# Third attention: TensorE's sums placed later by the number of units that VectorE takes

## The chip, the cores and the metric

The kernel runs on one core of a Trainium2 chip (trn2). The metric is the device time of one execution in microseconds, here the median of three runs; lower is better. One further execution was recorded by the hardware profiler, and all rows below are of that one.

## The reference

The reference is a chain of eight layers on an activation of 4 batches x 1024 tokens x 128 channels in float32. The seventh layer, the third attention, is the one that the change acts on. It has 16 heads of 8 channels, and its queries and keys are the same centred tokens:

```python
xh = x.reshape(B, T, H, hd)
x_centered = xh - jnp.mean(xh, axis=1, keepdims=True)
corr = jnp.einsum('bthd,bThd->bhtT', x_centered, x_centered)
corr = jax.nn.softmax(corr, axis=-1)
out = jnp.einsum('bhtT,bThd->bthd', corr, xh)
```

The first and the third layer are attentions too (one with a slope bias on the scores, one with scores damped by distance); the others are feed-forward layers and a layer of fast weights. Each layer is added to the activation.

## The kernel before

The whole chain is one program; each layer is a block in which every engine has its own instruction stream, and streams meet only through semaphores. All three attentions use `attend_transposed` when the scores are small enough (the third one always).

**Units and places.** The 16 heads are taken in 4 head groups (`HG`) of 4 heads (`GH`), for each of 4 batches. Within a head group there are 8 key tiles `J` of 128 keys (`JT`), so 32 units (`UNITS`); unit n = 4J + j is head j against key tile J, a tile of 128 keys x 1024 queries. `ORDER` says which unit stands at which place of the program. In the third attention `given=(31,)`: unit 31 is not exponentiated by ScalarE but computed by VectorE as a power of two (a range split and a polynomial, `take_power`, `round_power`, `raise_two`), and it stands at place 2. So units 0 and 1 are at places 0 and 1, and unit n from 2 to 30 is at place n + 1.

**TensorE.** `scores(hg, place, b)` (L995, matmuls at L1012) writes a unit's scores, two matmuls of 512 queries that run side by side, into one of three slots of PSUM (`s_ps`, `SLOTS = 3`), place modulo 3 over the batch's 128 places. It waits for the exponential of the unit that held the slot (`exped`), or for `powers_out` where that was VectorE's unit. As 128 is not a multiple of 3, the first three places of a batch take the slots of the last group's places 30, 31 and 29, in this order. `sum_up(hg, J, c, b)` (L1017, matmuls at L1036) multiplies the four tiles of key tile J by the values, for query half c (0 left, 1 right), and accumulates in `o_ps`; in the profile it is eight matmuls. The left half of J waits for the exponentials of all four units. For J = 0 both halves wait until VectorE has taken the last head group's sums out of `o_ps` (`o_out`), for J = 7 the left half waits for VectorE's unit (`raised_out`).

TensorE's order is written out by hand in `batch` (L1045): at each n from 0 to 31 it issues the scores of place n + 3 (of the next head group or batch from n = 29 on), and then, before the change,

```python
if n % GH == GH - 1:
    sum_up(hg, n // GH, 0, b)
if n % GH == 1:
    if n > GH:
        sum_up(hg, n // GH - 1, 1, b)
```

that is, the left half of J at n = 4J + 3 and the right half at n = 4J + 5; the right half of J = 7 comes at n = 1 of the next head group. Batch 0 and batch 3 are written out, batches 1 and 2 are a loop of the engine (`pe.Fori`).

**ScalarE.** `batch` (L1116) takes the places in order, one `Exp` of 128 x 1024 each (L1129), from `s_ps` into `probs`, which holds two key tiles (`J % 2`). Before the first unit of a key tile (j = 0) it waits for `summed`, which the right half of the sum of the key tile two back increments:

```python
if j == 0:
    act.wait_ge(summed, b * (HG * JT) + (hg * JT + J + 1))
```

`summed` starts at 2. For J = 0 of a head group this is the last head group's J = 6, for J = 1 it is its J = 7.

**VectorE** takes the next head group's unit out of its slot (`take_power`, L1174), copies the left and the right sums out of `o_ps` (`take_sums`, L1153) when `left_summed` and `summed` allow, and raises its unit. **GpSimd** copies the values of each head group (`v_set`) and scales finished batches. **SyncE** loads the queries and keys of the next head group after a count of `exped` and moves sums to DRAM.

Of the kernel before, what the change touches and what calls it, by code (L numbers as in the profile page):

```python
# [20 lines left out]
P = 128  # L21
D = 128
BATCH, SEQ = 4, 1024
# [769 lines left out]
def attend_transposed(nc, tag, V, operands, joined, ident, table=None, slopes=None, span=None, X=None, w_out=None,  # L793
# [10 lines left out]
    NB = HG * UNITS  # L804
    SLOTS = 3
    TAKE_AT = (4, 7)
    ORDER = [n for n in range(UNITS) if n not in given]
    KEPT = len(ORDER)
    NE = HG * KEPT
    NG = len(given)  # L810
    GIVEN_AT = (2, 15)[:NG]
    for place, n in zip(GIVEN_AT, given):
        ORDER.insert(place, n)
    RAISE = 7
    LATER = 6
    INVERT_AT = (22, 26)
# [6 lines left out]
    def part(h, J, c):  # L823

        lo, hi = span(h, J)
        lo, hi = max(lo, c * BANK), min(hi, (c + 1) * BANK)
        return (lo, hi) if lo < hi else None

    EARLY = 2 * (BATCH - 1)
    KNOWN = (HG - 1) * GH * HD  # L830
# [7 lines left out]
    with ExitStack() as stack:  # L838
# [7 lines left out]
        w_last = k.sb(f"{tag}_w_last", [P, D])  # L846
        spreader = k.sb(f"{tag}_spreader", [P, P])
        update = k.sb(f"{tag}_update", [P, 2, 4, D])
        if given:
            power = k.sb(f"{tag}_power", [P, SEQ])  # L850
            whole = k.sb(f"{tag}_whole", [P, SEQ], I32)
            raised = k.sb(f"{tag}_raised", [P, NG, SEQ])
            powers_out = k.sem(f"{tag}_powers_out")
            rounded = k.sem(f"{tag}_rounded")
            stepped = k.sem(f"{tag}_stepped")
            doubled = k.sem(f"{tag}_doubled")
            raised_out = k.sem(f"{tag}_raised_out")
# [33 lines left out]
        def _(sp):  # L891
# [32 lines left out]

            def ahead(b, hg):

                sp.wait_ge(exped, b * NE + ((hg - 1) * KEPT + SLOTS + (LATER if hg == 1 else 0)))
                operands.load(sp, hg % HG, b + hg // HG)

            def batch(b, first, final):  # L930
# [60 lines left out]
        def _(pe):  # L991
            pe.sem_inc(summed, 2)

            def scores(hg, place, b):
                J, j = divmod(ORDER[place], GH)  # L995
                half = hg % 2
                if place == 0:
                    pe.wait_ge(loaded[half], b * (HG // 2 * operands.all_in) + (hg // 2 + 1) * operands.all_in)
                at = hg * UNITS + place
                back = at - SLOTS if at >= SLOTS else max(m for m in range(-SLOTS, 0) if slot(0, m + NB) == slot(0, at))  # L1000
                of, was = divmod(back, UNITS)
                if ORDER[was] in given:
                    pe.wait_ge(powers_out, b * (NG * HG) + (of * NG + given.index(ORDER[was]) + 1))
                else:
                    pe.wait_ge(exped, b * NE + (of * KEPT + ORDER[was] + 1 + SLOTS))
                for c in range(2):
                    if not part(hg * GH + j, J, c):
                        continue
                    left, right = part(hg * GH + j, J, c)
                    tile = int(c != J // (JT // 2)) if by_dve else c  # L1010
                    rows = slice(PAIR_ROW * tile, PAIR_ROW * tile + operands.depth(tile))
                    last = pe.matmul(s_ps[:, slot(hg, place), left:right], k_rows[rows, half, j, J * P:(J + 1) * P],  # L1012
                                     q_rows[rows, half, j, left:right], start=True, stop=True)
                last.then_inc(scored, 1)

            def sum_up(hg, J, c, b):
                if J == 0:  # L1017
                    pe.wait_ge(o_out, b * (2 * HG) + (2 * hg + 3 + c))
                if c == 0:
                    if J == 0:  # L1020
                        pe.wait_ge(v_set, b * HG + (hg + 1))
                    pe.wait_ge(exped, b * NE + (hg * KEPT + min(GH * (J + 1), KEPT) + SLOTS))
                    if given and J == JT - 1:
                        pe.wait_ge(raised_out, b * (NG * HG) + (hg + 1) * NG)
                for j in range(GH):
                    h = hg * GH + j
                    meets = [i for i in range(JT) if part(h, i, c)]
                    if J not in meets:
                        continue
                    left, right = part(h, J, c)  # L1030
                    seen = part(h, J - 1, c)[1] if J > meets[0] else left
                    pieces = [(lo, hi) for lo, hi in ((left, min(seen, right)), (seen, right)) if lo < hi]
                    for lo, hi in pieces:
                        n = J * GH + j
                        weights = raised[:, given.index(n), lo:hi] if n in given else probs[:, J % 2, j, lo:hi]
                        last = pe.matmul(o_ps[VW * j:VW * (j + 1), c, lo - c * BANK:hi - c * BANK],  # L1036
                                         v_cols[:, hg % 2, J, j, :], weights,
                                         start=(J == meets[0]),
                                         stop=(J == meets[-1] and hi == right))
                if c == 1:  # L1040
                    last.then_inc(summed, 1)
                elif J == JT - 1:
                    last.then_inc(left_summed, 1)

            def batch(b, first, final):  # L1045
                for hg in range(HG):
                    for n in range(UNITS):
                        m = n + SLOTS
                        if m < UNITS:
                            scores(hg, m, b)  # L1050
                        elif hg + 1 < HG:
                            scores(hg + 1, m - UNITS, b)
                        elif not final:
                            scores(0, m - UNITS, b + 1)

                        if n % GH == GH - 1:
                            sum_up(hg, n // GH, 0, b)
                        if n % GH == 1:
                            if n > GH:
                                sum_up(hg, n // GH - 1, 1, b)  # L1060
                            elif hg:
                                sum_up(hg - 1, JT - 1, 1, b)
                            elif not first:
                                sum_up(HG - 1, JT - 1, 1, b - 1)
                if final:
                    sum_up(HG - 1, JT - 1, 1, b)

            for n in range(SLOTS):
                scores(0, n, 0)
# [42 lines left out]
        def _(act):  # L1112
# [2 lines left out]

            def batch(b):  # L1116
                for hg in range(HG):
                    for place, n in enumerate(ORDER):
                        if n in given:
                            continue  # L1120
                        J, j = divmod(n, GH)
                        lo, hi = span(hg * GH + j, J)
                        if by_dve:
                            act.wait_ge(adjusted, b * NE + (hg * KEPT + n + 1))
                        else:
                            act.wait_ge(scored, b * NB + (hg * UNITS + place + 1))
                        if j == 0:
# [13 lines left out]
        def _(dve):  # L1141
# [29 lines left out]
            def take_power(b, hg, i):  # L1171

                dve.wait_ge(scored, b * NB + (hg * UNITS + GIVEN_AT[i] + 1))
                dve.tensor_scalar(power[:, :], s_ps[:, slot(hg, GIVEN_AT[i]), :], LOG2_E, -126.0,  # L1174
                                  ALU.mult, ALU.max).then_inc(powers_out, 1)

            def round_power(b, hg, i):
                at = b * (NG * HG) + (hg * NG + i)
# [3 lines left out]
                dve.tensor_copy(whole[:, :], power[:, :]).then_inc(rounded, 1)  # L1182

            def raise_two(b, hg, i):
                at = b * (NG * HG) + (hg * NG + i)
                done = b * (NG * HG * RAISE) + (hg * NG + i) * RAISE
                rest, acc = power[:, :], raised[:, i, :]
# [35 lines left out]
            def batch(b, first, final):  # L1223
                for hg in range(HG):
                    if not by_dve:
                        if final and hg == HG - 1:
                            invert(b, 0, 1)
                            invert(b, 1, 1)
                        following = given and not (final and hg == HG - 1)
# [4 lines left out]
                        if following:  # L1234
                            round_power(*after, 0)
                        take_sums(b, hg, 1)
                        if following:
# [4 lines left out]
                        for i in range(1, NG if following else 1):  # L1242
                            take_power(*after, i)
# [17 lines left out]
            for i in range(NG):  # L1261
                take_power(0, 0, i)
                round_power(0, 0, i)
                raise_two(0, 0, i)
# [240 lines left out]
def centred_attention(nc, tag, X, ident, parts_dram, shift_dram, const, head_of):  # L1505
# [6 lines left out]
    with ExitStack() as stack:  # L1512
# [4 lines left out]
        norm_and_centre(nc, f"{tag}_split", X, XN, parts_dram, shift_dram, head_of, operands, ident)  # L1517
        joined = k.sb(f"{tag}_joined", [P, TOK])
        attend_transposed(nc, f"{tag}_att", XN, operands, joined, ident, X=X, kept=const.kept_sums,
                          given=(TPB * GH - 1,))  # L1520


def norm_and_centre(nc, tag, X, XN, parts_dram, shift_dram, head_of, operands, ident):
# [1474 lines left out]
```

## Time and profile before

| | us |
|---|---|
| median of three runs | 3316.86 |
| lowest and highest of them | 3312.75, 3324.0 |
| the profiled execution, its own time | 3323.09 |
| its span, first to last instruction | 3321.4 |
| mean granted TensorE clock over the span | 0.941 |
| third attention, first exponential to last | 2779 to 3244 |

The span is what the rows' times count from. The profiled execution was 6.2 us slower than the median of the runs. PE is TensorE, ACT ScalarE, DVE VectorE, POOL GpSimd, SP SyncE. Exponentials overlap at their edges, so a row that merges several has a length below their sum.

### The profile page before, as it was taken

How to read it: one execution, taken by the hardware profiler on the slowest of the kernel's cores; microseconds unless marked ns; L12 is line 12 of the kernel's file. 1: busy time of each engine (PE TensorE's matmuls, PEld its weight loads, DVE VectorE, ACT ScalarE, POOL GpSimd, SP SyncE). 2: the span in 40 equal slices, each digit the busy share in tenths (PEclk: the TensorE clock that was granted, in tenths of full speed). 3: DMA queues.
4: the chain of work that ended last, by engine and by line, in shares of the span. 5: the costliest groups of instructions: out<-in, count | busy, mean ns of one | idle time of the engine just before them, and what ended most of it. 6: DMA issues, size and time to landing. Idle time of an engine off the chain costs nothing. (4 is left out here: it accounts for less than half of the span.)

```text
span 3321.4 us, 53185 instructions
## 1 busy us (share of the span) xinstructions
PE 2874.0 (87%) x17952; PEld 1294.0 (39%) x17952; DVE 2340.6 (70%) x3805; ACT 2377.6 (72%) x3572; POOL 224.3 (7%) x180
## 2 busy tenths in 40 slices
PE   4888888899999578888889999979979756888886
PEld 2221222666776311111147666732237551111115
DVE  6777777677776767777767777779999855443454
ACT  5889889555455679999955555556635657999994
POOL 2000000000000310000010000010000011000002
PEclk8899999999999789999989999989979967999997
DMA  5444552000000544544300000000000004233321
GB/s 130 66 61 59 68 69 42 26 0 1 0 0 1 140 81 59 66 56 65 53 32 0 0 0 0 0 28 1 1 1 0 0 22 104 40 56 47 57 49 28
DMA packets 79832, 125.47 MB, mean 38 GB/s; under 512 B 12984, under 2 KB 32344, under 8 KB 78748
## 3 DMA queue, kind: packets, MB, share of 16 engines
q1 hardware_dynamic: 79612, 122.65, 21.8%
q8 instruction: 125, 2.05, 0.3%
q14 instruction: 95, 0.78, 0.1%
HBM read 87.49 MB, written 29.16 MB: 35 GB/s over the span
## 5 line engine op out<-in xcount | busy, mean ns | idle before, releaser
L1952 ACT ACTIVATE m_mix_hidden<-m_mix_up_ps 128x512 f32<-128x512 f32 x512 | 305.7, 597 | 295.1 <-PE m_mix_up_ps L1868 295.1
L1129 ACT ACTIVATE b_direct_probs<-b_direct_s_ps 128x1024 f32<-128x1024 f32 x512 | 473.6, 1091 | 18.2 <-PE b_direct_o_ps L1036 11.9
L1876 PE MATMUL m_mix_down_ps<-m_w,m_mix_hidden 128*128 128x128 f32 x4096 | 474.8, 276 | 0.0
L1876 PEld LDWEIGHTS m_mix_down_ps<-m_w,m_mix_hidden 128*128 128x128 f32 x4096 | 467.2, 192 | 15.3 <-issue 15.3
L1868 PE MATMUL m_mix_up_ps<-m_mix_ZT,m_w 128*128 128x512 f32 x1024 | 471.8, 619 | 0.0
L1129 ACT ACTIVATE a_direct_probs<-a_direct_s_ps 128x1024 f32<-128x1024 f32 (+10 forms) x512 | 431.8, 938 | 54.7 <-DVE a_direct_s_ps L1167 41.9
L1129 ACT ACTIVATE c_att_probs<-c_att_s_ps 128x1024 f32<-128x1024 f32 x496 | 457.9, 1141 | 6.8 <-PE c_att_s_ps L1012 4.2
L1167 DVE SCALAR_TENSOR_TENSOR a_direct_s_ps<-distance,slopes,a_direct_s_ps 128x512 f32<-128x512 f32 (+3 forms) x512 | 355.3, 732 | 117.7 <-PE a_direct_s_ps L1012 114.7
L1164 DVE TENSOR_TENSOR b_direct_s_ps<-b_direct_s_ps,distance 128x512 f32<-128x512 f32 x512 | 335.8, 695 | 141.9 <-PE b_direct_s_ps L1012 141.0
L1036 PE MATMUL c_att_o_ps<-c_att_probs,c_v_cols 128*32 128x512 f32 x1984 | 274.9, 610 | 50.2 <-ACT c_att_probs L1129 50.2
L1036 PE MATMUL b_direct_o_ps<-b_direct_probs,v_cols 128*32 128x512 f32 x2048 | 275.1, 610 | 14.0 <-DVE b_direct_taken L1153 13.1
L1036 PE MATMUL a_direct_o_ps<-a_direct_probs,v_cols 128*32 128x512 f32 (+12 forms) x2168 | 270.4, 550 | 16.3 <-DVE a_direct_taken L1153 14.9
L1868 PEld LDWEIGHTS m_mix_up_ps<-m_mix_ZT,m_w 128*128 128x128 f32 x1024 | 157.5, 190 | 291.1 <-ACT m_mix_hidden L1952 274.1
L2071 DVE TENSOR_REDUCE m_mix_mixed<-m_mix_weighted 128x128 f32<-128x1024 f32 x128 | 246.9, 1929 | 4.4
L1012 PE MATMUL b_direct_s_ps<-b_q_rows,b_k_rows 48*128 48x512 bf16 x1024 | 198.3, 392 | 47.5 <-ACT b_direct_probs L1129 15.7
L1012 PE MATMUL a_direct_s_ps<-a_q_rows,a_k_rows 48*128 48x512 bf16 (+13 forms) x984 | 194.2, 380 | 50.1 <-ACT a_direct_probs L1129 22.5
L1174 DVE TENSOR_SCALAR c_att_power<-c_att_s_ps 128x1024 f32<-128x1024 f32 x16 | 19.6, 1225 | 237.7 <-PE c_att_s_ps L1012 237.7
L1012 PE MATMUL c_att_s_ps<-c_q_rows,c_k_rows 49*128 49x512 bf16 x1024 | 162.7, 388 | 19.2 <-ACTq L1113 11.9
L2068 DVE TENSOR_TENSOR m_mix_weighted<-m_mix_down_ps,m_mix_combine 128x1024 f32<-128x1024 f32 x128 | 156.4, 1222 | 30.0 <-PE m_mix_down_ps L1876 24.6
L1012 PEld LDWEIGHTS b_direct_s_ps<-b_q_rows,b_k_rows 48*128 48x128 bf16 x1024 | 47.7, 93 | 332.7 <-ACT b_direct_probs L1129 321.0
L1012 PEld LDWEIGHTS a_direct_s_ps<-a_q_rows,a_k_rows 48*128 48x128 bf16 (+1 forms) x984 | 46.7, 94 | 289.5 <-ACT a_direct_probs L1129 261.2
L2330 DVE TENSOR_TENSOR f_recur_dots_prods<-f_recur_dots_vecs 128x1024 f32<-128x1024 f32 (+2 forms) x128 | 153.8, 1216 | 0.0
(385 smaller groups left out, 3498.5 us busy)
## 6 DMA issues: line engine op xcount, KB each, us to landing
qk_parts<-b_qkv_parts SPq DMA_DIRECT2D x48, 256.0 KB, 3.5
qk_parts<-a_qkv_parts SPq DMA_DIRECT2D x24, 256.0 KB, 4.9
a_k_rows<-qk_parts SPq DMA_DIRECT2D x32, 192.0 KB
a_q_rows<-qk_parts SPq DMA_DIRECT2D x32, 192.0 KB
b_k_rows<-qk_parts SPq DMA_DIRECT2D x32, 192.0 KB
b_q_rows<-qk_parts SPq DMA_DIRECT2D x32, 192.0 KB
qk_parts<-c_split_parts SPq DMA_DIRECT2D x24, 256.0 KB, 3.0
c_k_rows<-qk_parts SPq DMA_DIRECT2D x32, 192.0 KB
```

The source lines that it names most:

```text
L1012: last = pe.matmul(s_ps[:, slot(hg, place), left:right], k_rows[rows, half, j, J * P:(J + 1) * P], q_rows[rows, half, j, left:right], star ...
L1036: last = pe.matmul(o_ps[VW * j:VW * (j + 1), c, lo - c * BANK:hi - c * BANK], v_cols[:, hg % 2, J, j, :], weights, start=(J == meets[0]), ...
L1129: act.activation(probs[:, J % 2, j, lo:hi], s_ps[:, slot(hg, place), lo:hi], ACT.Exp).then_inc(exped, 1)
L1164: ins = dve.tensor_tensor(held, held, near, ALU.mult)
L1167: ins = dve.scalar_tensor_tensor(out=held, in0=near, scalar=slopes[:, h:h + 1], in1=held, op0=ALU.mult, op1=ALU.add)
L1174: dve.tensor_scalar(power[:, :], s_ps[:, slot(hg, GIVEN_AT[i]), :], LOG2_E, -126.0, ALU.mult, ALU.max).then_inc(powers_out, 1)
L1868: pe.matmul(up_ps[:, f % UP_BANKS, :], w["w1"][:, f * P:(f + 1) * P], ZT[:, half, :], start=True, stop=True).then_inc(up_done, 1)
L1876: last = pe.matmul(down_ps[:, t % 2, e, :], hidden[:, e * HALVES + h, t * P:(t + 1) * P], w["w2"][:, e * HALVES + h, :], start=(h == 0), s ...
L1952: act.activation(hidden[:, f, :], up_ps[:, f % UP_BANKS, :], ACT.Silu).then_inc(silu_done, 1)
L2068: dve.tensor_tensor(weighted[:, :, :], down_ps[:, t % 2, :, :], over(combine[:, half, t, :], D), ALU.mult).then_inc(down_out, 1)
L2071: dve.tensor_reduce(mixed[:, :], weighted[:, :, :].rearrange("p e d -> p d e"), AX, ALU.add).then_inc(summed, 1)
L2330: dve.tensor_tensor(prods[:, r % 2, at + lo:at + hi, :], vecs[:, r % 2, lo:hi, :], vecs[:, r % 2, other:other + 1, :].to_broadcast([P, hi ...
```

## The change

Two things are done to `attend_transposed`. First, the units given to VectorE may differ from head group to head group (`given` is a tuple of tuples), with the counts of semaphores taken from running sums (`KEPT`, `GIVEN`); the third attention passes unit 31 for each of the four head groups, and the other two pass none. With these arguments every count comes out as before, and VectorE's program is the same. Second, `sums_at` places TensorE's sums: the halves of J stand at n = 4J + 3 + g and 4J + 5 + g, where g is the number of units that the head group gives to VectorE. That is 1 in the third attention and 0 in the others. So in the third attention the left halves move from n = 4J + 3 to 4J + 4 and the right halves from 4J + 5 to 4J + 6; the two halves of J = 7 stand at n = 0 and n = 2 of the next head group (after the last batch they are issued at the end).

```diff
-    ORDER = [n for n in range(UNITS) if n not in given]
-    KEPT = len(ORDER)
-    NE = HG * KEPT
-    NG = len(given)
-    GIVEN_AT = (2, 15)[:NG]
-    for place, n in zip(GIVEN_AT, given):
-        ORDER.insert(place, n)
+    given = given or ((),) * HG
+    GIVEN_AT = (2, 6)
+    ORDER = [[n for n in range(UNITS) if n not in units] for units in given]
+    KEPT = [sum(len(order) for order in ORDER[:hg]) for hg in range(HG + 1)]
+    NE = KEPT[HG]
+    GIVEN = [sum(len(units) for units in given[:hg]) for hg in range(HG + 1)]
+    NG = GIVEN[HG]
+    for order, units in zip(ORDER, given):
+        for place, n in zip(GIVEN_AT, units):
+            order.insert(place, n)
...
+    def sums_at(hg, n):
+
+        return [(past, J, c) for past in (1, 0) for J in range(JT) for c in range(2)
+                if n + past * UNITS == J * GH + (GH - 1, GH + 1)[c] + len(given[(hg - past) % HG])]
...
-                        if n % GH == GH - 1:
-                            sum_up(hg, n // GH, 0, b)
-                        if n % GH == 1:
-                            if n > GH:
-                                sum_up(hg, n // GH - 1, 1, b)
-                            elif hg:
-                                sum_up(hg - 1, JT - 1, 1, b)
+                        for past, J, c in sums_at(hg, n):
+                            if hg >= past:
+                                sum_up(hg - past, J, c, b)
                             elif not first:
-                                sum_up(HG - 1, JT - 1, 1, b - 1)
+                                sum_up(HG - 1, J, c, b - 1)
                 if final:
-                    sum_up(HG - 1, JT - 1, 1, b)
+                    for n in range(GH + 2):
+                        for past, J, c in sums_at(HG, n):
+                            if past:
+                                sum_up(HG - 1, J, c, b)
...
         attend_transposed(nc, f"{tag}_att", XN, operands, joined, ident, X=X, kept=const.kept_sums,
-                          given=(TPB * GH - 1,))
+                          given=((TPB * GH - 1,),) * (HEADS // GH))
```

## Rows read from the trace of the kernel before

**Rows 1.** Page, first part: busy time, share, instructions of each engine.
```profile
PE 2874.0 (87%) x17952; PEld 1294.0 (39%) x17952; DVE 2340.6 (70%) x3805; ACT 2377.6 (72%) x3572; POOL 224.3 (7%) x180
```
**Rows 2.** Busy time by stretch: us, each engine, PEclk, DMA share, GB/s.
```profile
2779.00:3244.00 465.00, 407.54 (x3058) 79.54 (x3058) 211.76 (x214) 458.08 (x498) 25.49 (x18) 0.99 0.32 50
```
**Rows 3.** Page, costliest groups: busy, mean ns; idle before, releaser.
```profile
L1129 ACT ACTIVATE c_att_probs<-c_att_s_ps 128x1024 f32<-128x1024 f32 x496 | 457.9, 1141 | 6.8 <-PE c_att_s_ps L1012 4.2
...
L1036 PE MATMUL c_att_o_ps<-c_att_probs,c_v_cols 128*32 128x512 f32 x1984 | 274.9, 610 | 50.2 <-ACT c_att_probs L1129 50.2
```
**Rows 4.** Timeline of ScalarE, third attention: start, length, merged instructions, idle before.
```profile
2785.62 1.94 ACT L1129 ACTIVATE c_att_probs<-c_att_s_ps 128x1024 f32<-128x1024 f32 x2 [0.83 <-PE c_att_s_ps L1012]
2788.25 107.13 ACT L1129 ACTIVATE c_att_probs<-c_att_s_ps 128x1024 f32<-128x1024 f32 x116 [0.68 <-PE c_att_s_ps L1012]
...
3011.26 1.94 ACT L1129 ACTIVATE c_att_probs<-c_att_s_ps 128x1024 f32<-128x1024 f32 x2 [0.59 <-PE c_att_o_ps L1036]
3015.12 3.77 ACT L1129 ACTIVATE c_att_probs<-c_att_s_ps 128x1024 f32<-128x1024 f32 x4 [1.93 <-PE c_att_s_ps L1012]
3019.68 108.96 ACT L1129 ACTIVATE c_att_probs<-c_att_s_ps 128x1024 f32<-128x1024 f32 x118 [0.79 <-PE c_att_s_ps L1012]
3129.23 114.62 ACT L1129 ACTIVATE c_att_probs<-c_att_s_ps 128x1024 f32<-128x1024 f32 x124 [0.59 <-PE c_att_o_ps L1036]
```
**Rows 5.** ScalarE's timeline, single exponentials: places 29, 30, 31, then 0', 4', 5'.
```profile
3039.60 1.28 ACT L1129 ACTIVATE c_att_probs<-c_att_s_ps 128x1024 f32<-128x1024 f32 x1
3040.50 1.29 ACT L1129 ACTIVATE c_att_probs<-c_att_s_ps 128x1024 f32<-128x1024 f32 x1
3041.44 1.27 ACT L1129 ACTIVATE c_att_probs<-c_att_s_ps 128x1024 f32<-128x1024 f32 x1
3042.68 1.02 ACT L1129 ACTIVATE c_att_probs<-c_att_s_ps 128x1024 f32<-128x1024 f32 x1
...
3045.43 1.02 ACT L1129 ACTIVATE c_att_probs<-c_att_s_ps 128x1024 f32<-128x1024 f32 x1
3046.50 1.02 ACT L1129 ACTIVATE c_att_probs<-c_att_s_ps 128x1024 f32<-128x1024 f32 x1
```
**Rows 6.** TensorE's timeline at the same seam; the 3042.77 row from a narrower window.
```profile
3041.01 0.61 PE L1012 MATMUL c_att_s_ps<-c_q_rows,c_k_rows 49*128 49x512 bf16 x4
3041.54 1.07 PE L1036 MATMUL c_att_o_ps<-c_att_probs,c_v_cols 128*32 128x512 f32 x8
3042.54 0.61 PE L1012 MATMUL c_att_s_ps<-c_q_rows,c_k_rows 49*128 49x512 bf16 x4
3042.77 0.38 PE L1012 MATMUL c_att_s_ps<-c_q_rows,c_k_rows 49*128 49x512 bf16 x2
...
3044.99 0.63 PE L1036 MATMUL c_att_o_ps<-c_att_probs,c_v_cols 128*32 128x512 f32 x3
...
3045.99 0.61 PE L1012 MATMUL c_att_s_ps<-c_q_rows,c_k_rows 49*128 49x512 bf16 x4
```
**Rows 7.** VectorE's timeline at the same seam: the first step on its unit.
```profile
3043.19 1.23 DVE L1174 TENSOR_SCALAR c_att_power<-c_att_s_ps 128x1024 f32<-128x1024 f32 x1 [16.04 <-PE c_att_s_ps L1012]
```
**Rows 8.** Timelines of ScalarE (place 31) and TensorE, seam from batch 1 to 2.
```profile
3009.40 1.27 ACT L1129 ACTIVATE c_att_probs<-c_att_s_ps 128x1024 f32<-128x1024 f32 x1
3009.81 0.39 PE L1012 MATMUL c_att_s_ps<-c_q_rows,c_k_rows 49*128 49x512 bf16 x2 [0.45 <-ACT c_att_probs L1129]
3010.13 1.07 PE L1036 MATMUL c_att_o_ps<-c_att_probs,c_v_cols 128*32 128x512 f32 x8
...
3014.70 0.61 PE L1012 MATMUL c_att_s_ps<-c_q_rows,c_k_rows 49*128 49x512 bf16 x4 [1.97 <-issue]
```
**Rows 9.** Busy time by stretch as in rows 2, and one sum at its start.
```profile
2779.00:2788.00 9.00, 7.60 (x36) 1.02 (x32) 8.15 (x9) 7.72 (x10) 0.00 (x0) 0.52 0.22 44
...
3011.00:3020.00 9.00, 7.03 (x48) 1.19 (x48) 5.99 (x8) 6.03 (x7) 1.23 (x1) 0.81 0.01 4
2783.11 1.94 PE L1036 MATMUL c_att_o_ps<-c_att_probs,c_v_cols 128*32 128x512 f32 x8 [0.40 <-ACT c_att_probs L1129]
```

More of the change, by code:

```diff
@@ L848, in attend_transposed @@
         update = k.sb(f"{tag}_update", [P, 2, 4, D])
-        if given:
-            power = k.sb(f"{tag}_power", [P, SEQ])
+        if NG:
+            power = k.sb(f"{tag}_power", [P, max(len(units) for units in given), SEQ])
             whole = k.sb(f"{tag}_whole", [P, SEQ], I32)
-            raised = k.sb(f"{tag}_raised", [P, NG, SEQ])
+            raised = k.sb(f"{tag}_raised", [P, max(len(units) for units in given), SEQ])
             powers_out = k.sem(f"{tag}_powers_out")
@@ L925, in ahead @@
             def ahead(b, hg):
[L927 removed]
+                sp.wait_ge(exped, b * NE + (KEPT[hg - 1] + SLOTS + (LATER if hg == 1 else 0)))
                 operands.load(sp, hg % HG, b + hg // HG)
@@ L994, in scores @@
             def scores(hg, place, b):
-                J, j = divmod(ORDER[place], GH)
+                J, j = divmod(ORDER[hg][place], GH)
                 half = hg % 2
@@ L1001, in scores @@
                 of, was = divmod(back, UNITS)
-                if ORDER[was] in given:
-                    pe.wait_ge(powers_out, b * (NG * HG) + (of * NG + given.index(ORDER[was]) + 1))
+                unit = ORDER[of][was]
+                if unit in given[of]:
+                    pe.wait_ge(powers_out, b * NG + (GIVEN[of] + given[of].index(unit) + 1))
                 else:
-                    pe.wait_ge(exped, b * NE + (of * KEPT + ORDER[was] + 1 + SLOTS))
+                    pe.wait_ge(exped, b * NE + ((KEPT[of] if of >= 0 else KEPT[HG - 1] - NE) + unit + 1 + SLOTS))
                 for c in range(2):
@@ L1021, in sum_up @@
                         pe.wait_ge(v_set, b * HG + (hg + 1))
-                    pe.wait_ge(exped, b * NE + (hg * KEPT + min(GH * (J + 1), KEPT) + SLOTS))
-                    if given and J == JT - 1:
-                        pe.wait_ge(raised_out, b * (NG * HG) + (hg + 1) * NG)
+                    pe.wait_ge(exped, b * NE + (min(KEPT[hg] + GH * (J + 1), KEPT[hg + 1]) + SLOTS))
+                    if given[hg] and J == JT - 1:
+                        pe.wait_ge(raised_out, b * NG + GIVEN[hg + 1])
                 for j in range(GH):
@@ L1034, in sum_up @@
                         n = J * GH + j
-                        weights = raised[:, given.index(n), lo:hi] if n in given else probs[:, J % 2, j, lo:hi]
+                        weights = raised[:, given[hg].index(n), lo:hi] if n in given[hg] else probs[:, J % 2, j, lo:hi]
                         last = pe.matmul(o_ps[VW * j:VW * (j + 1), c, lo - c * BANK:hi - c * BANK],
@@ L1117, in batch @@
                 for hg in range(HG):
-                    for place, n in enumerate(ORDER):
-                        if n in given:
+                    for place, n in enumerate(ORDER[hg]):
+                        if n in given[hg]:
                             continue
@@ L1123, in batch @@
                         if by_dve:
-                            act.wait_ge(adjusted, b * NE + (hg * KEPT + n + 1))
+                            act.wait_ge(adjusted, b * NE + (KEPT[hg] + n + 1))
                         else:
@@ L1173, in take_power @@
                 dve.wait_ge(scored, b * NB + (hg * UNITS + GIVEN_AT[i] + 1))
-                dve.tensor_scalar(power[:, :], s_ps[:, slot(hg, GIVEN_AT[i]), :], LOG2_E, -126.0,
+                dve.tensor_scalar(power[:, i, :], s_ps[:, slot(hg, GIVEN_AT[i]), :], LOG2_E, -126.0,
                                   ALU.mult, ALU.max).then_inc(powers_out, 1)
             def round_power(b, hg, i):
-                at = b * (NG * HG) + (hg * NG + i)
+                at = b * NG + (GIVEN[hg] + i)
                 dve.wait_ge(powers_out, at + 1)
@@ L1181, in round_power @@
                     dve.wait_ge(raised_out, at)
-                dve.tensor_copy(whole[:, :], power[:, :]).then_inc(rounded, 1)
+                dve.tensor_copy(whole[:, :], power[:, i, :]).then_inc(rounded, 1)
             def raise_two(b, hg, i):
-                at = b * (NG * HG) + (hg * NG + i)
-                done = b * (NG * HG * RAISE) + (hg * NG + i) * RAISE
-                rest, acc = power[:, :], raised[:, i, :]
+                at = b * NG + (GIVEN[hg] + i)
+                done = b * (NG * RAISE) + (GIVEN[hg] + i) * RAISE
+                rest, acc = power[:, i, :], raised[:, i, :]
                 dve.wait_ge(rounded, at + 1)
@@ L1228, in batch @@
                             invert(b, 1, 1)
-                        following = given and not (final and hg == HG - 1)
+                        following = NG and not (final and hg == HG - 1)
                         after = (b, hg + 1) if hg + 1 < HG else (b + 1, 0)
@@ L1236, in batch @@
                         take_sums(b, hg, 1)
+                        for i in range(1, len(given[after[1]]) if following else 1):
+                            take_power(*after, i)
                         if following:
@@ L1241, in batch @@
                             invert(b - 1, 1)
-                        for i in range(1, NG if following else 1):
-                            take_power(*after, i)
+                        for i in range(1, len(given[after[1]]) if following else 1):
                             round_power(*after, i)
@@ L1259, in batch @@
                                 invert(b, INVERT_AT.index(n), 1)
-            for i in range(NG):
+            for i in range(len(given[0])):
                 take_power(0, 0, i)
```

## The prediction

> **What bounds the kernel now.** I read the page first: no engine is busy all the time, TensorE 87%, ScalarE 72% [rows 1], so the stage has to be taken by itself. The diff acts only on the third attention, where units are given to VectorE: the first two pass an empty tuple, for which every place, count and wait works out as before. The third one's exponentials run from 2779 to 3244 us, and there the stretch shows ScalarE busy 458 of 465 us and TensorE 408 at a granted clock of 0.99 [rows 2]. The costliest groups say how the two meet: TensorE's sums sat idle 50.2 us for the exponentials, ScalarE only 6.8 us in all [rows 3]. ScalarE sets the end of this stage; TensorE has room, but it runs in program order, and what stands behind a waiting instruction is late with it.
>
> ScalarE's own timeline has seven gaps that the profile counts [rows 4]. Two (0.83, 0.68) follow the slow first microseconds, two (1.93, 0.79) follow the jump of TensorE's loop, and three (0.59 in the row shown, 0.68, 0.59) stand where a batch begins. All that TensorE's order could give back there is 0.83 + 0.68 + 1.93 + 0.79 = 4.2 us.
>
> The smaller losses don't count as gaps, since exponentials overlap; they show in the ends. Call the places of a head group 0 to 31, the next group's 0' to 31'. Exponentials of places 30 and 31 end at 3041.79 and 3042.71, 0.92 apart, ScalarE's steady pace. That of 0' ends at 3043.70, 0.99 later: 0.07 lost. Those of 4' and 5' end at 3046.45 and 3047.52, 1.07 apart: 0.15 lost [rows 5]. So 0.22 us is lost at each seam between head groups. Why: place 0' is unit 0, which writes the half of `probs` that the sum of J = 6 reads, and it waits for `summed`. The right half of that sum begins at 3041.54 [rows 6], ends 1.07 later, and 0' is dispatched at 3042.68 [rows 5]. Place 5' is unit 4, which waits for the sum of J = 7, begun at 3044.99 and ended near 3046.05, and for its scores, issued behind it at 3045.99 and done 0.39 later [rows 6].
>
> **The change.** Nothing is added or removed in instructions on ScalarE, VectorE, GpSimd or SyncE; the DMAs and their queue's waits get the same counts. Only TensorE's sums move, each half one place later: the left from 4J + 3 to 4J + 4, the right from 4J + 5 to 4J + 6. What each passes is one `scores` (two matmuls) with its wait. For unit 4J + 3, which sits at place 4J + 4, this fits: the left half used to hold back the next scores while it waited, and no longer does. The 50.2 us of idle time before the sums [rows 3] shrink, but that idle time is TensorE's. ScalarE's seven gaps are its only chance to gain.
>
> The price is on the release of `probs`. Steps from the rows: TensorE sees an exponential's end 0.06 us later (3042.71, then scores at 3042.77), a sum is issued 0.31 behind scores (3009.81 to 3010.13), the next issue is 1.00 behind a half sum (3041.54 to 3042.54), scores to scores 0.23 (two places issued from 3042.54, the second at 3042.77), and 0' is dispatched 1.14 behind the half sum's start [rows 5, 6, 8].
>
> *Seam inside a batch (12 of them).* The right half of J = 6 now stands at n = 30, behind the scores of place 33 (1'), which need the slot of place 30: 3041.79 + 0.06 = 3041.85. The half sum goes at 3042.16 instead of 3041.54, and 0' is dispatched at 3043.30 and ends at 3044.32. Without loss it would be 3042.71 + 0.92 = 3043.63: 0.69 lost where 0.07 was. What is late next: scores of 2' go at 3043.16; VectorE's first step on its unit follows 0.43 behind and takes 1.23 [rows 7], so it is done by 3044.82, in time. Scores of 3' wait for 0': 3044.38. The left half of J = 7 now stands behind them, 3044.69. Scores of 4' follow at 3045.69, and 4' is dispatched at 3046.12. With 1' and 3' ending at 3045.24 and 3046.16 (0.92 apart behind 0'), 4' was due by 3046.05 (its end at 3047.07 less 1.02): 0.07 lost. Scores of 5' go at 3045.92, the right half of J = 7 at 3046.23, and 5' is dispatched at 3046.23 + 1.14 = 3047.37, or 0.08 later if its two waits cost what they do now (scores done at 3046.38, dispatch at 3046.50, where 0.04 is usual). Its end at 3048.47 is 0.41 behind 3047.14 + 0.92. The seam loses 0.69 + 0.07 + 0.41 = 1.17 against 0.22, +0.95 with the 0.08 and +0.87 without it; I take +0.93, nearer the former, since the 0.08 is there now. Twelve make **11.2 us**.
>
> *Seam between batches (3).* 128 places on three slots don't divide, so scores of 0' wait there for place 30 and those of 1' for place 31. Before, the right half of J = 6 starts behind the former, at 3010.13, and 0' at 3011.26 [rows 4, 8]. Now it stands behind the latter: place 31 ends at 3010.67, so 3011.04, +0.91. The rest of the seam adds the 0.48 of 4' and 5' for the 0.15 there is now: +1.24 each, **2.5 us** for two. At the third TensorE's loop jumps back, 1.97 us idle behind its last half sum, scores of 3' at 3014.70 [rows 8]. Now the jump stands behind the scores of 2', which slip to 3012.04 and last 0.39; with 1.97 idle the scores of 3' come at 3014.4 or a little later, no later than before, and the 1.93 us gap absorbs the late 0'. But two half sums follow before the scores of 5' and 6' where one did: **+0.7**, with 1.5 either way, since a clock drop falls right there [rows 9]. SyncE's loads for the next head group wait for a count of exponentials and are late only with them.
>
> *Inside a head group (6 sums of 16 groups).* The right half now frees `probs` at E + 0.06 + 0.31 + 1.14 = E + 1.51, where E is the end of place 4J - 2; unit 4J of two tiles on is due to be dispatched at E + 2 x 0.92 - 0.10 = E + 1.73. (0.10 is 1.02 less 0.92.) 0.22 us of room covers it, and I cost it at nothing; if that room is gone, each tenth lost costs 96 x 0.1 = 9.6 us.
>
> *Start and end of the stage.* In the cold first group scores of 7 come sooner, the release of place 9 later: 0.0, within 1. At the end nothing changes: there are no scores left to pass, and both halves of J = 7 wait for the last exponential and follow it as before.
>
> Sum: 11.2 + 2.5 + 0.7 = **+14.4 us**. Against the profiled execution (span 3321.4, its own time 3323.09) that is 3337.5; the three runs' median is 3316.86, 6.2 lower, and I predict against it: **3331.3 us**, 0.43% slower. Bounds: nothing lost but the gaps given back, -4.2; all seams with 1.17 + 0.1 and the interior with a lost tenth, +26.
>
> **The rivals.** *Not slower.* If 0' were held by its scores and not by the sum, the change would only give back gaps: 0 to 4.2 us, 3312.7 to 3316.9. For it: the exponentials' starts run ahead of their ends by up to 0.27 us (1.29 against 1.02 long [rows 5]). Against: 0' starts 0.07 behind the end of the half sum, its scores were issued by 3041.24, and the profile names the sum as releaser at the batch seam [rows 4]. It decides if the half sum can start by 3043.63 - 1.02 - 1.14 = 3041.47; I have 3042.16.
>
> *Only the first wait bites.* If 5' is hidden by what 0' already lost: 12 x 0.62 + 3 x 0.91 = 10.2, less up to 4.2 of gaps: 3323 to 3327. My walk leaves 5' 0.3 short after the earlier delay was counted, which speaks against it.
>
> *The interior stalls too.* If ScalarE's pace is that of its starts, 0.90 us (3039.60 to 3040.50 [rows 5]), the release comes at start + 1.26 + 1.51 = 2.77 against 3 x 0.90 = 2.71. That is 0.06 us lost 96 times, 5 to 6 us more: 3337. For it: the starts do run at 0.90. Against: a duration that grows from 1.02 to 1.29 while ends stay 0.92 apart says the starts run ahead of the work. The Trainium skill, "Perfetto Trace Analysis", section "DVE / Act Engine Instruction", has the profiled start as the moment when the instruction leaves the queue and begins to execute; by that rule this rival would hold, and the growing durations speak against it here.
>
> *The clock falls.* TensorE gets shorter, evenly spread holes in place of one long one. The granted clock is 0.52 in the first 9 us, 0.81 in the 9 us around the loop's jump [rows 9] and 0.99 over the whole [rows 2]; at the lower of its two levels, 1.2 GHz, a sum's eight matmuls take 1.94 us and not 1.07 [rows 6, 9]. Four places would then need about 2 x 1.86 + 4 x 0.4 = 5.4 us where ScalarE needs 3.7: 1.7 us lost per four places, 20 us if one of ten fours fell there, 3351. TensorE's total work is unchanged and each hole gets shorter, so it is unlikely. The Trainium skill, "TensorE: Matmul & The Clock Gate", section "A second HAM failure mode: psum-queue depth-cycling", reports a kernel whose small idles between groups of matmuls let the clock oscillate; the present kernel has such idles and holds 0.99, so the trace doesn't agree so far.
>
> **How the numbers follow.** Chances: forecast 0.70 (3331.3, by itself 3326 to 3336), only the first wait 0.10, not slower 0.08, interior 0.08, clock 0.04. The range reaches into the second and the fourth: 3323 to 3339. 0.3% (10 us) is about what this measurement tells from no change, so slower begins at 3326.8: most of the forecast's 0.70 and the last two, 0.79; same 0.18; faster 0.03.
>
> **What the profile after would show.** Ends 30 to 0' at a seam inside a batch some 1.6 us apart (0.99 before), 4' to 5' 1.2 to 1.35, starts inside a group still 0.90 apart; a head group 29.5 to 29.6 us long where four of them take 114.62 [rows 4], 28.65 each; idle time before sums waiting for exponentials well under 50 us; ScalarE's idle in the stage up by more than 10 us and put down to the sums' tile; PEclk unchanged. The prediction is wrong if 0' keeps its distance to 31, if the interior starts spread, or if PEclk falls.

## The result: slower, by the wait and at the places that were forecast

Five runs of each kernel gave medians of 3338.65 us after (3336.01 to 3347.7) and 3319.62 us before, a ratio of 1.0059 with a 95% interval of 1.0044 to 1.0073. The changed kernel was then run again beside a larger number of runs of the kernel before (8 against 31): 3333.8 against 3323.02 us, 1.0039 (1.0022 to 1.0055). The forecast was 1.0043 (+14.4 us). Direction and cause were right. The trace of the changed kernel is 12.9 us longer than the one of before (3334.3 against 3321.4), and what the third attention adds to it is shown by the same view as [rows 2], here with the stretch cut exactly from the first exponential's start to the last one's end. Columns: stretch, us, busy time and instructions of TensorE, its weight loads, VectorE, ScalarE, GpSimd, then PEclk, DMA share, GB/s. First the kernel before:

```profile
575.00:2779.21 2204.21, 1944.36 (x11272) 1037.64 (x11272) 1663.42 (x2864) 1411.61 (x2369) 134.79 (x103) 0.94 0.14 27
2779.21:3243.85 464.64, 407.24 (x3052) 79.44 (x3050) 211.76 (x214) 457.88 (x497) 25.49 (x18) 0.99 0.32 50
3243.85:3321.40 77.55, 52.65 (x332) 45.61 (x332) 39.36 (x75) 29.13 (x94) 17.27 (x11) 0.75 0.11 30
```

and the changed kernel:

```profile
575.00:2776.34 2201.34, 1941.58 (x11264) 1033.63 (x11256) 1663.25 (x2864) 1411.36 (x2369) 134.81 (x103) 0.94 0.14 27
2776.34:3254.93 478.59, 433.87 (x3052) 86.55 (x3050) 212.97 (x214) 459.46 (x497) 25.57 (x18) 0.99 0.30 49
3254.93:3334.30 79.37, 54.87 (x332) 47.81 (x332) 39.37 (x75) 29.33 (x94) 17.26 (x11) 0.71 0.10 29
```

The stage went from 464.64 to 478.59 us, **+13.95** where +14.4 was forecast. Everything ahead of it was 2.9 us shorter and everything behind 1.8 us longer, in code that the change doesn't touch. Same instructions, the same clock, and ScalarE's busy time up by 1.6 us only: ScalarE waits longer. TensorE's busy time rose by 27 us without a matmul more, because two `scores` in a row count 0.61 us and two apart 0.39 each; it is no sign of more work.

The page of the changed kernel, the groups that answer to [rows 3] (line numbers are 8 or 9 higher):

```profile
L1137 ACT ACTIVATE c_att_probs<-c_att_s_ps 128x1024 f32<-128x1024 f32 x496 | 459.5, 1143 | 19.1 <-PE c_att_o_ps L1045 16.6
L1045 PE MATMUL c_att_o_ps<-c_att_probs,c_v_cols 128*32 128x512 f32 x1984 | 275.0, 610 | 0.5 <-ACT c_att_probs L1137 0.5
```

TensorE's idle time before sums fell from 50.2 us to 0.5, and ScalarE's idle time rose from 6.8 to 19.1, of which 16.6 is put down to the sums. Most of what TensorE no longer waited before its sums it waited before its scores instead, as the groups of the scores say, before and after:

```profile
L1012 PE MATMUL c_att_s_ps<-c_q_rows,c_k_rows 49*128 49x512 bf16 x1024 | 162.7, 388 | 19.2 <-ACTq L1113 11.9
```
```profile
L1021 PE MATMUL c_att_s_ps<-c_q_rows,c_k_rows 49*128 49x512 bf16 x1024 | 196.3, 392 | 54.9 <-ACT c_att_probs L1137 20.9
```

So 49.7 us of waiting went away in one place and 35.7 came back in the other. All of it belonged to the engine that had time to spare.

ScalarE's timeline of the changed kernel, answering to [rows 4] (start, length, merged instructions, idle before):

```profile
2811.36 24.86 ACT L1137 ACTIVATE c_att_probs<-c_att_s_ps 128x1024 f32<-128x1024 f32 x27 [0.21 <-PE c_att_o_ps L1045]
2836.81 3.85 ACT L1137 ACTIVATE c_att_probs<-c_att_s_ps 128x1024 f32<-128x1024 f32 x4 [0.59 <-PE c_att_o_ps L1045]
2840.87 24.86 ACT L1137 ACTIVATE c_att_probs<-c_att_s_ps 128x1024 f32<-128x1024 f32 x27 [0.21 <-PE c_att_o_ps L1045]
2866.32 3.85 ACT L1137 ACTIVATE c_att_probs<-c_att_s_ps 128x1024 f32<-128x1024 f32 x4 [0.59 <-PE c_att_o_ps L1045]
2870.38 24.86 ACT L1137 ACTIVATE c_att_probs<-c_att_s_ps 128x1024 f32<-128x1024 f32 x27 [0.21 <-PE c_att_o_ps L1045]
2896.74 3.85 ACT L1137 ACTIVATE c_att_probs<-c_att_s_ps 128x1024 f32<-128x1024 f32 x4 [1.51 <-PE c_att_o_ps L1045]
...
3015.71 1.94 ACT L1137 ACTIVATE c_att_probs<-c_att_s_ps 128x1024 f32<-128x1024 f32 x2 [1.51 <-PE c_att_o_ps L1045]
3018.43 1.02 ACT L1137 ACTIVATE c_att_probs<-c_att_s_ps 128x1024 f32<-128x1024 f32 x1 [0.79 <-PE c_att_s_ps L1021]
3020.84 1.02 ACT L1137 ACTIVATE c_att_probs<-c_att_s_ps 128x1024 f32<-128x1024 f32 x1 [1.39 <-PE c_att_s_ps L1021]
3022.58 1.94 ACT L1137 ACTIVATE c_att_probs<-c_att_s_ps 128x1024 f32<-128x1024 f32 x2 [0.71 <-PE c_att_o_ps L1045]
```

What stood hidden in merged rows before is now cut at every seam: a gap of 0.59 us before place 0' and one of 0.21 us before place 5', both behind a sum. A head group is 2866.32 - 2836.81 = 29.51 us long; before it was 28.65 [rows 4]. At a seam between batches the first gap is 1.51, as the scores of 1' wait one exponential longer there. One seam as single exponentials, places 31, 0', 4' and 5', answering to [rows 5]:

```profile
3075.69 1.25 ACT L1137 ACTIVATE c_att_probs<-c_att_s_ps 128x1024 f32<-128x1024 f32 x1
3077.53 1.02 ACT L1137 ACTIVATE c_att_probs<-c_att_s_ps 128x1024 f32<-128x1024 f32 x1 [0.59 <-PE c_att_o_ps L1045]
3080.36 1.03 ACT L1137 ACTIVATE c_att_probs<-c_att_s_ps 128x1024 f32<-128x1024 f32 x1
3081.60 1.02 ACT L1137 ACTIVATE c_att_probs<-c_att_s_ps 128x1024 f32<-128x1024 f32 x1 [0.21 <-PE c_att_o_ps L1045]
```

and TensorE at the same seam, answering to [rows 6]:

```profile
3075.57 0.91 PE L1021 MATMUL c_att_s_ps<-c_q_rows,c_k_rows 49*128 49x512 bf16 x4
3076.40 1.07 PE L1045 MATMUL c_att_o_ps<-c_att_probs,c_v_cols 128*32 128x512 f32 x8
3077.40 0.39 PE L1021 MATMUL c_att_s_ps<-c_q_rows,c_k_rows 49*128 49x512 bf16 x2
...
3080.47 0.63 PE L1045 MATMUL c_att_o_ps<-c_att_probs,c_v_cols 128*32 128x512 f32 x3
```

The ends of 31 and 0' are 76.94 and 78.55, 1.61 apart (0.99 before), and 0' is dispatched 1.13 behind the right half of J = 6 (3076.40), as in the walk. Place 5' follows the right half of J = 7 (3080.47) by 1.13 too, and its end is 1.23 behind that of 4' (1.07 before). The end of 4' itself is 1.00 behind that of 3', where the steady distance is 0.92: its scores now stand behind the left half of J = 7. Read by the ends, a seam loses 0.69 at 0', 0.08 at 4' and 0.31 at 5', where it lost 0.07 at 0' and 0.15 at 5' before.

### The profile page after: what moved, and what is told of

It is laid out like the page before. It is cut to its first block and busy times, and to the rows that moved or that the text cites. A ratio compares the mean times of both kernels' runs of the same rounds, so it can differ in the third digit from the quotient of the medians.

```text
span 3334.3 us, 53185 instructions
## 1 busy us (share of the span) xinstructions
PE 2900.5 (87%) x17952; PEld 1300.1 (39%) x17952; DVE 2343.5 (70%) x3805; ACT 2379.1 (71%) x3572; POOL 224.3 (7%) x180
## 5 line engine op out<-in xcount | busy, mean ns | idle before, releaser
L1137 ACT ACTIVATE c_att_probs<-c_att_s_ps 128x1024 f32<-128x1024 f32 x496 | 459.5, 1143 | 19.1 <-PE c_att_o_ps L1045 16.6
L1045 PE MATMUL b_direct_o_ps<-b_direct_probs,v_cols 128*32 128x512 f32 x2048 | 275.2, 610 | 13.9 <-DVE b_direct_taken L1161 12.9
L1021 PE MATMUL c_att_s_ps<-c_q_rows,c_k_rows 49*128 49x512 bf16 x1024 | 196.3, 392 | 54.9 <-ACT c_att_probs L1137 20.9
L1182 DVE TENSOR_SCALAR c_att_power<-c_att_s_ps 128x1024 f32<-128x1024 f32 x16 | 19.6, 1224 | 237.1 <-PE c_att_s_ps L1021 237.1
L1021 PEld LDWEIGHTS c_att_s_ps<-c_q_rows,c_k_rows 49*128 49x128 bf16 x1024 | 46.6, 93 | 338.2 <-ACT c_att_probs L1137 314.9
```

The lines of the kernel that those rows point to most:

```text
L1137: act.activation(probs[:, J % 2, j, lo:hi], s_ps[:, slot(hg, place), lo:hi], ACT.Exp).then_inc(exped, 1)
L1182: dve.tensor_scalar(power[:, i, :], s_ps[:, slot(hg, GIVEN_AT[i]), :], LOG2_E, -126.0, ALU.mult, ALU.max).then_inc(powers_out, 1)
```

## The experiments

My theory was that only the two releases of `probs` (the moments at which a finished sum lets ScalarE write that half again) at a seam cost time: that of place 0' by the right half of J = 6, and that of 5' by the right half of J = 7. The rivals were that every late sum costs (work, interior), and that the runs' +19.6 us hold something outside the stage. All kernels differ from the changed one in the condition in `sums_at` or in the number of key tiles that `probs` holds. The length of the stage in each trace tells them apart better than ratios do, which are uncertain by 0.1 to 0.15%.

**The changed kernel again** (no edit).

> The changed kernel itself, once more. The traces explain +13.9 us: the stage from the first exponential to the last is 478.6 us long after and 464.6 before. The five runs say 1.0059 (+19.6). If those traces are the whole of it, the ratio comes out near 1.0042 (+14), with the stage at 478.6 again. If the other 5 us are real and lie outside the stage, the ratio is near 1.006 again and some other stretch of the trace is longer than before.

1.0039 (1.0022 to 1.0055), and the stage in its trace:

```profile
2774.27:3253.23 478.96, 433.82 (x3052) 86.49 (x3050) 212.99 (x214) 459.46 (x497) 25.50 (x18) 0.99 0.31 49
```

The stage is 478.96 against 478.59, so it repeats to 0.4 us, and the ratio now agrees with what the stage adds (13.95 of 3321.4 is 0.42%). The first set's extra 5 us did not come back.

**One sum of the eight right halves put back.**

```diff
-  ... + len(given[(hg - past) % HG])]
+  ... + (len(given[(hg - past) % HG]) if (J, c) != (JT - 2, 1) else 0)]
```

> The changed kernel with one sum of eight put back: the right half of J = 6 at 4J + 5, all others late. Theory (the late release of probs at the seams sets the time): place 0' is released as before, only 5' is late behind the right half of J = 7. Steps as in the prediction give about +6 us against before (8 less than the changed kernel), stage 470 to 471 us, gap before 0' gone. Rival (every late sum costs alike, by work or by the interior): about 14 x 15/16 = +13, stage 477 to 478.

1.0027 (1.0014 to 1.004), 3328.02 us; its stage, and two rows of ScalarE's timeline:

```profile
2775.89:3246.93 471.04, 431.26 (x3052) 86.23 (x3050) 213.00 (x214) 459.47 (x497) 25.73 (x18) 0.99 0.31 49
```
```profile
2810.39 28.78 ACT L1137 ACTIVATE c_att_probs<-c_att_s_ps 128x1024 f32<-128x1024 f32 x31 [0.21 <-PE c_att_o_ps L1045]
2839.39 28.78 ACT L1137 ACTIVATE c_att_probs<-c_att_s_ps 128x1024 f32<-128x1024 f32 x31 [0.21 <-PE c_att_o_ps L1045]
```

One half sum in sixteen takes back 7.6 of the 13.95 us, and inside a batch the gap before 0' is gone from the rows while that before 5' stays, 31 exponentials apart. A head group is 29.00 us long. Place 0' isn't quite where it was: its end still comes 0.18 late where 0.07 was lost before, since the left half of J = 6 now stands directly ahead of the right half.

**The late places only inside a head group, J = 0 to 5.**

```diff
+  ... + (len(given[(hg - past) % HG]) if J < JT - 2 else 0)]
```

> The sums of J = 0 to 5 late, both halves of J = 6 and J = 7 where they were before. Theory: nothing is lost inside a head group, 0.22 us of room covers it, and the jump of the loop is as before: -1 to 0 us, stage 464 to 465 us, ratio 1.000, starts inside a group 0.90 apart. Rival (the interior pays too, or the idle time of TensorE before sums was worth something): three quarters of the change, +5 or more, or a gain of over 3 us.

1.0009 (0.9997 to 1.0022). The stage, the group of the sums, and ScalarE's timeline over one undisturbed batch:

```profile
2779.15:3243.34 464.19, 430.18 (x3052) 86.16 (x3050) 211.73 (x214) 458.06 (x497) 25.46 (x18) 0.99 0.31 50
```
```profile
L1045 PE MATMUL c_att_o_ps<-c_att_probs,c_v_cols 128*32 128x512 f32 x1984 | 274.5, 609 | 2.3 <-ACT c_att_probs L1137 0.4
```
```profile
3128.72 114.62 ACT L1137 ACTIVATE c_att_probs<-c_att_s_ps 128x1024 f32<-128x1024 f32 x124 [0.59 <-PE c_att_o_ps L1045]
```

Three quarters of the sums are late and a batch is 114.62 us long, to the hundredth what it was [rows 4]. Nothing is lost inside a group. How near it comes shows at unit 28, the last of a group that waits for a release. The half sum that releases it, and the exponentials of units 26, 27 and 28, each merged with the one behind it:

```profile
2862.13 1.06 PE L1045 MATMUL c_att_o_ps<-c_att_probs,c_v_cols 128*32 128x512 f32 x8
2861.42 2.17 ACT L1137 ACTIVATE c_att_probs<-c_att_s_ps 128x1024 f32<-128x1024 f32 x2
2862.33 2.18 ACT L1137 ACTIVATE c_att_probs<-c_att_s_ps 128x1024 f32<-128x1024 f32 x2
2863.27 2.16 ACT L1137 ACTIVATE c_att_probs<-c_att_s_ps 128x1024 f32<-128x1024 f32 x2
```

Unit 28 starts 1.14 behind the half sum and 0.94 behind unit 27, so its start was held by the release; the ends of 27, 28 and 29 (2863.59, 2864.51, 2865.43) are 0.92 apart all the same. The idle time before sums is down from 50.2 us to 2.3, and the stage gains 0.45 us by it, all of it around the first group and the loop's jump.

**Only J = 6 and J = 7 late.**

```diff
+  ... + (len(given[(hg - past) % HG]) if J >= JT - 2 else 0)]
```

> Only the sums of J = 6 and J = 7 late, J = 0 to 5 where they were before; the opposite half of the run that moved only those. Theory: the seams are the whole price, so this one costs as much as the changed kernel, +14 us against before, stage 478 to 479 us, though only a quarter of the sums moved. Rival (each late sum costs alike): +3.5, stage 468.

1.0032 (1.0019 to 1.0045).

```profile
2779.22:3256.24 477.02, 407.26 (x3052) 80.25 (x3050) 213.03 (x214) 459.47 (x497) 25.29 (x18) 0.99 0.31 49
```
```profile
2809.87 3.85 ACT L1137 ACTIVATE c_att_probs<-c_att_s_ps 128x1024 f32<-128x1024 f32 x4 [0.59 <-PE c_att_o_ps L1045]
2813.94 24.86 ACT L1137 ACTIVATE c_att_probs<-c_att_s_ps 128x1024 f32<-128x1024 f32 x27 [0.21 <-PE c_att_o_ps L1045]
2839.38 3.85 ACT L1137 ACTIVATE c_att_probs<-c_att_s_ps 128x1024 f32<-128x1024 f32 x4 [0.59 <-PE c_att_o_ps L1045]
```

A quarter of the sums carries +12.4 of the +13.95 us, with the same two gaps and the same 29.51 us per head group. The stage is 1 to 2 us shorter than I expected. The 1.6 us between it and the changed kernel's lie in the first head group and in the one behind the loop's jump, the two stretches where [rows 9] have the clock low.

**Left halves late, right halves as before.**

```diff
+  ... + (len(given[(hg - past) % HG]) if c == 0 else 0)]
```

> All left halves late (4J + 4), all right halves where they were (4J + 5), so between the two there is one place of scores and not two. Theory: the right half of J = 6 and of J = 7 are then held up behind their left half, not behind scores, and stand half a step later than before: +7 us, stage 471 to 472. Rival (the left halves are what the time gains or loses nothing by): 464 to 465.

1.0019 (1.0009 to 1.0028).

```profile
2784.40:3255.80 471.40, 415.00 (x3052) 87.43 (x3050) 212.71 (x214) 459.45 (x497) 25.69 (x18) 0.99 0.31 49
```

+6.8 us with no right half moved, as much as expected, but only in part by the wait that I expected. The page and a row of ScalarE's timeline name the scores:

```profile
L1137 ACT ACTIVATE c_att_probs<-c_att_s_ps 128x1024 f32<-128x1024 f32 x496 | 459.4, 1154 | 12.0 <-PE c_att_s_ps L1021 9.2
```
```profile
2848.19 28.78 ACT L1137 ACTIVATE c_att_probs<-c_att_s_ps 128x1024 f32<-128x1024 f32 x31 [0.37 <-PE c_att_s_ps L1021]
```

Scores of 5' stand behind both halves of J = 7 here, and 5' waits for them; by the ends it loses 0.48, 0' only 0.18 and 4' 0.08. So a late half sum has two ways to ScalarE: by the `probs` that it frees, and by the scores that stand behind it in TensorE's order. In the changed kernel it is the first way that costs at 0' and 5'. That the number came out as expected here is in part luck.

**Right halves late, left halves as before.**

```diff
+  ... + (len(given[(hg - past) % HG]) if c == 1 else 0)]
```

> All left halves where they were (4J + 3), all right halves late (4J + 6). Theory: 0' is released 0.6 us late as in the changed kernel, but the left half of J = 7 is out of the way earlier, so 4' and 5' lose little: +7.5 us, stage 471.5 to 473, with the gap before 0' as in the changed kernel and the one before 5' small. Rival (the right halves carry all of it): 478.

1.0017 (1.0003 to 1.0032).

```profile
2782.64:3253.49 470.85, 423.03 (x3052) 80.09 (x3050) 211.75 (x214) 456.64 (x497) 25.69 (x18) 0.99 0.31 49
```
```profile
2813.52 28.52 ACT L1137 ACTIVATE c_att_probs<-c_att_s_ps 128x1024 f32<-128x1024 f32 x31 [0.59 <-PE c_att_o_ps L1045]
2842.63 28.52 ACT L1137 ACTIVATE c_att_probs<-c_att_s_ps 128x1024 f32<-128x1024 f32 x31 [0.59 <-PE c_att_o_ps L1045]
```

+6.2 us, a little under the 7 to 8 expected. The gap before 0' is the changed kernel's and the one before 5' is gone: this kernel is the complement of the one with J = 6 put back (29.11 us per head group here, 29.00 there, 29.51 with both gaps, 28.65 with neither).

**`probs` for four key tiles, late places.** ScalarE then waits for the sum four key tiles back.

```diff
+    KEYS = 2 if by_dve else 4
-        probs = k.sb(f"{tag}_probs", [P, 2, GH, SEQ])
+        probs = k.sb(f"{tag}_probs", [P, KEYS, GH, SEQ])
-            pe.sem_inc(summed, 2)
+            pe.sem_inc(summed, KEYS)
...
-    ... probs[:, J % 2, j, lo:hi]
+    ... probs[:, J % KEYS, j, lo:hi]
-    dve.wait_ge(summed, b * (HG * JT) + (hg * JT + JT + 2))
+    dve.wait_ge(summed, b * (HG * JT) + (hg * JT + JT + KEYS))
```

> The changed kernel with probs for four key tiles and not two in the third attention, so that an exponential waits for the sum four tiles back; the places of all sums as in the changed kernel. Theory: with the wait on probs gone both seam losses go, and what is left is the order's small gain: -2 us against before, stage 462 to 463 us, no gap at the seams but 0 to 0.6 at the batches. Rival (the late sums cost TensorE's time, or the slots of the scores are what is late): stays near +14, stage 475 or more.

0.9994 (0.9979 to 1.0009).

```profile
2781.03:3242.87 461.84, 430.44 (x3052) 86.32 (x3050) 213.00 (x214) 456.49 (x497) 25.19 (x18) 0.99 0.31 50
```
```profile
L1138 ACT ACTIVATE c_att_probs<-c_att_s_ps 128x1024 f32<-128x1024 f32 x496 | 456.5, 1183 | 5.3 <-PE c_att_s_ps L1022 5.3
```

With every sum where the change put it, the stage is 16.75 us shorter than the changed kernel's, and the page puts none of ScalarE's idle time down to the sums. What is left of a seam is the 0.08 at place 4', which waits for its scores. So the late sums cost next to nothing in themselves; the wait on the buffer that they free is nearly the whole price.

**`probs` for four key tiles, places of before** (the edit above and `len(...)` times 0).

> The kernel before's places for all sums, with probs for four key tiles. Theory: its 0.22 us at each seam was the same wait and goes too: -2 us against before, stage 462 to 463. With the wait gone the place of the sums hardly matters: within 1 us of the late placement with four key tiles (stage 461.8). Rival (the late placement is better by its own once the buffer is gone): over 3 us apart.

0.9998 (0.9982 to 1.0014).

```profile
2781.36:3244.55 463.19, 404.92 (x3052) 79.01 (x3050) 211.76 (x214) 457.40 (x497) 25.67 (x18) 0.99 0.32 50
```

1.35 us longer than with the late places, where within 1 was expected. Some 0.3 us of it is in each batch (124 exponentials in 114.32 us, against 123 in 113.08, with 0.92 for the one more); the first group is slower here (gaps of 0.83 and 0.81 us against one of 0.36) and the jump quicker (one gap of 3.07 us against 2.61 and 1.38). So the late places may gain a little by themselves once the buffer is out of the way; one trace of each, with jumps that differ this much, doesn't show more. Both versions with four key tiles have a shorter stage than the kernel before, by 2.8 and 1.45 us, and neither can be told from it by the time of the whole.

## Why the prediction was right, and where its number was off

*What bounds the stage*: right. ScalarE sets it, and nothing that only shortened TensorE's idle time moved the end by more than half a microsecond (the run with late interiors).

*Seams inside a batch, 12 x 0.93 = 11.2*: measured 29.51 - 28.65 = 0.86 each, 10.3. The ends of 31 and 0' lie 1.61 apart as stated. The 0.08 that I added for the double wait of 5' was not paid: it was dispatched 1.13 behind the half sum. With it left out, my walk gives 0.87. (Where the prediction says what the profile would show, "ends 30 to 0'" are those of 31 and 0'.)

*Seams between batches and the jump, 2.5 + 0.7*: what is left of 13.95 is 3.6, against 3.2. By the ends, the two seams between batches lose 2.2 more than before and the first head group 0.1, and the jump 1.2 where 0.7 was forecast: scores of 3' came when they should, but the left half of J = 7, which now stands behind them and ahead of the scores of 4', took 1.93 us, and the right half 1.34, where 1.07 is usual. Before, the left half was through ahead of the jump, and the half sum that took 1.94 us came only behind the scores of 6'. The 0.92 from waiting for place 31 shows in the gap, 1.51 against 0.59. Around the jump three gaps of 0.79, 1.39 and 0.71 follow each other where two stood.

*Inside a head group, nothing*: right, and shown by the run that moved only those. That refutes the interior rival. Its sum was near the truth for the starts, the last of which the release did hold; its step from a late start to a late end was wrong. The Trainium skill, "Perfetto Trace Analysis", section "DVE / Act Engine Instruction", has the profiled start as the moment when the instruction begins to execute, and the profiled end as the one when its writes have been acknowledged. The prediction took the first half to bear the rival out; the section doesn't say what a late start costs. The run with late interiors does: a batch of 114.62 us and not 1.4 us more (24 times 0.06).

*The other rivals*: "not slower" fell: 16.6 us of ScalarE's idle time are put down to the sums, and the buffer experiment removes them. "Only the first wait bites" fell: with the first taken back, 6.4 us stay. The stage's clock was 0.99 in every kernel, with long holes, short ones or fewer; what the Trainium skill reports in "TensorE: Matmul & The Clock Gate", section "A second HAM failure mode: psum-queue depth-cycling", did not happen here.

*The total*: here the number was off, 3331.3 for 3338.65. The step that failed is the base of the sum. I set the +14.4 on the median of three runs, 3316.86, though the profiled execution had taken 3323.09. The five runs of the kernel before have a median of 3319.62, the later 31 of 3323.02 and a further 34 of 3323.96: the base was 2.8 to 7.1 us too low. The added term held in the stage (13.95, and 14.3 in the repeat), but not in the first runs' medians, which lie 19.0 apart; those of the repeat lie 10.8 apart.

The record has something on those first five. It lists each execution's mean granted clock. In the 65 later executions of the kernel before, the four at 0.939 took 3325.1 to 3331.4 us and the seven at 0.945 or 0.946 took 3311.5 to 3316.2; a line through all of them falls by some 2.3 us for each 0.001. The changed kernel's first five had 0.936 to 0.941, 0.939 in the mean, the eight of the repeat 0.9415 (for the five of the kernel before no clocks are listed). By that line, an estimate, the difference in clock is worth 5.7 us, and at equal clock the two sets lie 11 and 10 us above the kernel before. So the first set's excess went with a lower clock outside what the change does (the same kernel didn't have it in the repeat). That is a correlation; no run shows what lowered the clock, nor why 10 to 11 us are left of the stage's 14.

## What to carry to other kernels

Before a step of an in-order engine is moved to spare that engine a wait, look up what the step releases, and on which engine: here TensorE's 50 us of waiting in front of its sums went, most of them only to stand in front of its scores, and ScalarE, which has no room, paid 14 us for it. A release has its slack at each place of the loop separately, 0.22 us inside a group by the prediction's walk and less than none at the seam, so the seam is to be walked. In merged rows small stalls of an engine whose instructions overlap don't show as idle time; the distance of ends does.

## What the runs showed of the hardware

ScalarE's exponentials start 0.90 us apart and end 0.92 apart while nothing holds them, and their recorded length grows from 1.02 us behind a stall to 1.29 [rows 5]; with four key tiles it reached 1.37. A start that comes late by less than that growth costs nothing at the end, which is why a start that was 0.34 us late at the old seam (3042.68 for 3041.44 + 0.90) cost only 0.07. Unit 28 of the run with late interiors is the same case. This row shows the length grown in the kernel with four key tiles (place 3' of a seam):

```profile
2840.02 1.35 ACT L1138 ACTIVATE c_att_probs<-c_att_s_ps 128x1024 f32<-128x1024 f32 x1
```

The jump of TensorE's loop left it idle for 1.97 us in the kernel before [rows 8]; in the kernel with J = 6 put back, where it stands behind a `scores`, the row says 3.13, and in the one with late interiors, where it stands behind a sum as before, 2.13:

```profile
3014.02 0.39 PE L1021 MATMUL c_att_s_ps<-c_q_rows,c_k_rows 49*128 49x512 bf16 x2 [3.13 <-issue]
```
```profile
3014.47 0.61 PE L1021 MATMUL c_att_s_ps<-c_q_rows,c_k_rows 49*128 49x512 bf16 x4 [2.13 <-issue]
```

In the changed kernel, behind a `scores` too, it was 2.04, and 2.49 when the same kernel was run again. It isn't a constant, and single jumps differ by as much as the gains that were looked for here.
